# Fourth stage of a five-stage hybrid block: the product inside a chunk in 16-bit halves, ScalarE's input products, and a later output projection

## The chip, the cores and the metric

The kernel runs on one core of a Trainium2 chip. A core has TensorE (matrix products, into the eight PSUM banks), VectorE, ScalarE and GpSimd (elementwise work; GpSimd does not touch PSUM here) and a queue that starts DMAs. Each engine works through its own list of instructions in order and waits at semaphores for the others. The metric is the device time of one execution in microseconds (us), lower is better.

## The reference

The program applies five layers one after the other to 1024 tokens of 512 features: two scans over an image, a two-layer state-space block, a quantised linear layer, the state-space block that is changed here, and a mixture of experts. The changed layer computes this (`u` is the normalised input, 4 heads of 256 columns, state size 32):

```python
u_norm = u * jax.lax.rsqrt(jnp.mean(u * u, axis=-1, keepdims=True) + RMS_EPS) * norm_w
zxbcdt = u_norm @ in_proj_w.T + in_proj_b
...
dt = jax.nn.softplus(dt + dt_bias)
A = -jnp.exp(A_log)
dtA = jnp.exp(dt * A)
dtB = dt[..., None] * B_mat
def step(h, inp):
    dtA_t, dtB_t, x_t, C_t = inp
    h = h * dtA_t[:, :, None, None] + dtB_t[..., None] * x_t[:, :, None, :]
    y_t = jnp.einsum('bhn,bhnp->bhp', C_t, h)
    return (h, y_t)
...
y = y + x * D[None, None, :, None]
y = y.reshape(B, L, D_INNER)
y = y * jax.nn.silu(z)
return y @ out_proj_w.T + out_proj_b
```

## The kernel before

The five layers are five stages; every engine passes a common semaphore between two stages, so none starts a stage before all have ended the one before. All that follows is in the fourth, `stage_l3`, whose tiles have the prefix `ab_` in the profile. It holds the tokens in `t` and works through them in 8 chunks of 128, with the scan over time written as matrix products. `chunks` runs `body` for chunk 0, a loop over chunks 1 to 6, and chunk 7. There is one buffer of each tile for all chunks, and PSUM has a fixed use: bank 0 the output projection, bank 1 the projection to B and C and later the exponents, banks 2 and 3 x, the product inside the chunk and the transposed y, banks 4 and 5 z and the part from the state, banks 6 and 7 transposed B and C, B.C and the update of the state. The order on each engine is the order of the code; nothing else schedules it.

Big projections are done in halves: each 32-bit operand is the sum of two 16-bit tiles (`_hi`, `_lo`), and three 16-bit products (hi.hi, hi.lo, lo.hi) stand for one 32-bit product. Other products take 32-bit tiles as they are; the trace shows each of these as two records.

TensorE's list for a chunk, with the lines of the profile: transposes of B and C (L1679, 8); two products that give the differences of decay exponents (L1683, "the exponent product"); B.C per head (L1687, 4, only 32 rows deep); state times C (L1691, 4, 32 rows deep); the product inside the chunk, `M` times `xdt` (L1697, 4, 32-bit); the update of the state (L1702, 4, 32-bit); the next chunk's projection to B and C (L1644, 12 of 256 columns) and the first half of z (L1644, 12 of 512); transposes of y (L1712, 8); second half of z (12); the output projection (L1721, 24 of 512); the next chunk's x (L1644, 24 of 512).

Beside it, ScalarE copies the transposed B and C out (L1591), takes the exponential `E` (L1593), copies the transposed y out as its high half (L1595) and takes the tanh of z (L1580). VectorE masks B.C with the triangle (`gm`, L1478), forms `M = E * gm` (L1482), scales the state part (L1484), adds up y (L1489), gates it (L1491), adds to the state `S` (L1494), takes bc, the low half of y, z, the gate, the decays and x (L1438, L1498, L1442, L1446, L1457, L1451), multiplies x by dt (`xdt`, L1453), and last adds the output projection to `t` (L1510); the statistics of the chunk before are L1473. GpSimd forms `xe` (x times the decay to the chunk's end, L1612), `dx` (D times x, L1613), adds `dx` to y (L1617) and scales `S` (L1620).

## Time and profile before

| | us |
|---|---|
| runs: median (lowest, highest) | 1711.53 (1709.33, 1713.68), 3 runs |
| the profiled execution: its time | 1710.17 |
| the profiled execution: span of its instructions | 1708.4 |
| fourth stage, chunks 0 to 7 (917.3 to 1141.7 in the span) | 224.4 |
| TensorE busy in the whole span | 1363.5 (80%) |
| mean granted TensorE clock, whole span | 0.871 |

A page of the profile gives for each engine its busy time and, for groups of instructions of one line, their number, total and mean duration, and the idle time of the engine just before them with what ended it. The granted clock is a share of 2.4 GHz: 1.00 is that level, 0.50 is 1.2 GHz. Matrix products are pipelined: the duration of one has its way through the array in it, so in a dense row the distance from start to start counts, not the duration.

### The profile page before, as it was taken

What the parts mean: (1) busy time and instruction counts of PE and PEld (TensorE: products, weight loads), DVE (VectorE), ACT (ScalarE), POOL (GpSimd) and SP (SyncE); (2) the same over time, 40 slices, a digit from 0 to 9 for tenths busy, and PEclk for the clock granted to TensorE, in tenths of its full rate; (3) what the DMA queues carried; (4) which work ended last, traced back from release to release, by engine and by line L of the source; (5) the groups of instructions that cost most, each with busy time, mean ns of one, the idle gap of its engine ahead of it and who ended that gap; (6) DMA issues with size and microseconds to landing.
All of it is one profiled execution on the core that took longest, in us unless ns stands there. A gap on an engine that the chain in (4) does not pass through costs nothing.

```text
span 1708.4 us, 34435 instructions
## 1 busy us (share of the span) xinstructions
PE 1363.5 (80%) x12846; PEld 928.9 (54%) x12847; DVE 1109.4 (65%) x1669; ACT 671.5 (39%) x1011; POOL 417.0 (24%) x390
## 2 busy tenths in 40 slices
PE   3734889888548989884738999976699999999991
PEld 2214566665345666652425555544477777777770
DVE  3586877887578778876876555556456774667432
ACT  3236434344364343341252111124346664566330
POOL 0122333443313434432132323323100000000004
PEclk9757799999778899987858999885799999999996
DMA  8051000000220000003221000005543553535004
GB/s 293 18 173 61 2 2 1 1 1 1 80 82 2 2 1 1 1 1 105 93 83 50 0 0 0 0 4 209 193 183 142 218 217 114 218 126 219 25 25 153
DMA packets 34029, 132.30 MB, mean 77 GB/s; under 512 B 6665, under 2 KB 8457, under 8 KB 24017
## 3 DMA queue, kind: packets, MB, share of 16 engines
q1 hardware_dynamic: 25808, 103.19, 16.7%
q0 software_dynamic: 8160, 28.32, 4.9%
q8 instruction: 37, 0.61, 0.1%
q14 instruction: 24, 0.19, 0.0%
HBM read 108.82 MB, written 22.68 MB: 77 GB/s over the span
## 4 chain that ended last, share of the span: by engine, by line
PE 57%; DVE 24%; issue 7%; ACT 6%; DMA 4%; POOL 2%; DVEq 0%; POOLq 0%; SPq 0%; ACTq 0%
PE banks L2102 13%; PE banks L2123 13%; DVE mb_ca L592 8%; PE banks L1644 6%; PE banks L1003 5%; PE banks L1721 2%; PE banks L977 2%; PE banks L1040 2%; PE banks L1697 2%; PE banks L1050 2%; PE banks L1051 1%; ACT mb_ca L804 1%; POOL xs_table L2135 1%; DVE mb_xc L604 1%; DVE mb_y_lo L640 1%
## 5 line engine op out<-in xcount | busy, mean ns | idle before, releaser
L2102 PE MATMUL banks<-eb_x_hi,eb_w_hi 128*128 128x128 f16 x1344 | 228.3, 220 | 2.0 <-DVE eb_x_lo L2002 2.0
L2102 PE MATMUL banks<-eb_x_lo,eb_w_hi 128*128 128x128 f16 x1344 | 228.3, 220 | 0.0
L2102 PE MATMUL banks<-eb_x_hi,eb_w_lo 128*128 128x128 f16 x1344 | 228.3, 220 | 0.0
L977 PE MATMUL banks<-mb_u_hi,mb_wi_hi 128*128 (+3 forms) x1152 | 198.0, 220 | 3.3 <-ACT mb_ca L804 3.3
L977 PE MATMUL banks<-mb_u_hi,mb_wi_lo 128*128 (+3 forms) x1152 | 197.7, 220 | 0.0
L977 PE MATMUL banks<-mb_u_lo,mb_wi_hi 128*128 (+3 forms) x1152 | 197.6, 220 | 0.0
L592 DVE SCALAR_TENSOR_TENSOR mb_ca<-mb_xp,mb_par,mb_ca 128x128 f32<-128x128 f32 x384 | 162.9, 487 | 25.3 <-ACT mb_ca L804 23.3
L2102 PEld LDWEIGHTS banks<-eb_x_hi,eb_w_hi 128*128 128x128 f16 x1344 | 132.3, 98 | 4.8 <-issue 2.4
L2102 PEld LDWEIGHTS banks<-eb_x_lo,eb_w_hi 128*128 128x128 f16 x1344 | 132.3, 98 | 2.4
L2102 PEld LDWEIGHTS banks<-eb_x_hi,eb_w_lo 128*128 128x128 f16 x1344 | 132.3, 98 | 0.0
L2123 PE MATMUL banks<-eb_w_hi,eb_h_hi 128*128 x336 | 127.9, 381 | 0.4 <-issue 0.4
L2123 PE MATMUL banks<-eb_w_hi,eb_h_lo 128*128 x336 | 127.9, 381 | 0.0
L2123 PE MATMUL banks<-eb_w_lo,eb_h_hi 128*128 x336 | 127.9, 381 | 0.0
L977 PEld LDWEIGHTS banks<-mb_u_hi,mb_wi_hi 128*128 128x128 f16 (+1 forms) x1152 | 114.1, 99 | 9.4 <-issue 6.3
L1953 DVE TENSOR_TENSOR eb_hb<-banks,eb_b 128x512 f32<-128x512 f32 x84 | 57.4, 690 | 92.6 <-PE banks L2102 81.9
L977 PEld LDWEIGHTS banks<-mb_u_hi,mb_wi_lo 128*128 128x128 f16 (+1 forms) x1152 | 113.2, 98 | 1.7
L658 DVE TENSOR_TENSOR mb_M<-mb_E,banks 128x512 f32<-128x512 f32 x128 | 84.6, 683 | 44.5 <-ACT mb_E L851 44.5
L977 PEld LDWEIGHTS banks<-mb_u_lo,mb_wi_hi 128*128 128x128 f16 (+1 forms) x1152 | 113.2, 98 | 0.0
L851 ACT ACTIVATE mb_E<-banks 128x512 f32<-128x512 f32 x128 | 74.7, 597 | 91.0 <-PE banks L1051 87.8
L1992 DVE TENSOR_TENSOR eb_w_lo<-eb_raw,eb_w_hi 128x2048 f32 (+1 forms) x36 | 81.1, 2288 | 23.0 <-ACT eb_w_hi L1998 16.0
L2039 ACT ACT_TABLE_LOAD x21 | 26.9, 1283 | 170.4 <-DVE eb_hb L1953 170.4
L1960 DVE TENSOR_TENSOR eb_h_lo<-eb_hb,eb_h_hi 128x512 f16<-128x512 f32 x84 | 57.7, 687 | 37.8 <-ACT eb_h_hi L2041 37.6
(431 smaller groups left out, 3255.0 us busy)
## 6 DMA issues: line engine op xcount, KB each, us to landing
eb_raw<-e_w SPq DMA_DIRECT2D x36, 1024.0 KB, 4.8
eb_un<-e_w SPq DMA_DIRECT2D x28, 1024.0 KB, 7.2
mb_ring<-m_in_w SPq DMA_DIRECT2D x8, 1072.0 KB, 5.4
xs_table<-zero POOLq DMA_DIRECT2D x1, 6400.0 KB, 21.0
eb_xg<-xs_table POOLq DMA_DIRECT2D x23, 256.0 KB, 2.9
ys_table<-eb_y POOLq DMA_DIRECT2D x21, 256.0 KB, 6.5
ab_raw<-a_in_w SPq DMA_DIRECT2D x4, 1154.0 KB, 11.8
mb_ring<-m_out_w SPq DMA_DIRECT2D x4, 1024.0 KB, 5.3
```

Source lines behind the costliest of these rows:

```text
L592: x = e.scalar_tensor_tensor(out=ca[:, j, :], in0=xp[:, j, k:k + P], scalar=par[:, MB_CVW + 4 * j + k:MB_CVW + 4 * j + k + 1], in1=ca[:, j ...
L658: e.tensor_tensor(M[:, MB_HG * k:MB_HG * (k + 1), :], E[:, 512 * (k % MB_ER):512 * (k % MB_ER + 1)].rearrange("p (h t) -> p h t", h=MB_HG) ...
L851: e.activation(E[:, 512 * (k % MB_ER):512 * (k % MB_ER + 1)], ps[:, 3 + k % 2, :], ACT.Exp).then_inc(exped, 1)
L977: x = e.matmul(ps[0:width, bank, n * P:(n + 1) * P], a[:, k, f:f + width], b[:, k, ds(i * P, P)], start=(k == 0 and m == 0), stop=(k == KD ...
L1003: x = e.matmul(ps[:, 7, :], a[:, j, :], b[:, j, :], start=(j == 0 and m == 0), stop=(j == JD - 1 and m == 2))
L1040: x = e.transpose(ps[:, 5 + j // 4, (j % 4) * P:(j % 4 + 1) * P], xc[:, j, :], core.ident[:])
L1644: x = e.matmul(out, a[:, k, ds(i * P, P)], b[:, k, col:col + width], start=(k == 0 and m == 0), stop=(k == KD - 1 and m == 2))
L1953: e.tensor_tensor(hb[:, j % 2, :].rearrange("p (c n) -> p c n", c=EX_GB), ps[:, j, :].rearrange("p (c n) -> p c n", c=EX_GB), b1[:, ds(x, ...
L1960: e.tensor_tensor(h_lo[:, j, :], hb[:, j % 2, :], h_hi[:, j, :], ALU.subtract).then_inc(hlo_done, 1)
L1992: e.tensor_tensor(w_lo[:, side, n, :], raw[q], w_hi[:, side, n, :], ALU.subtract).then_inc(wlo_done, 1)
L2102: o = e.matmul(ps[:, j, c * P:(c + 1) * P], a[:, side, k, f * P:(f + 1) * P], b[:, k, :], start=(k == 0 and m == 0), stop=(k == KD - 1 and ...
L2123: o = e.matmul(ps[:, 5, :], a[:, j, c * P:(c + 1) * P], b[:, ds(side, 1), KD + j, c * D:(c + 1) * D].rearrange("p o c -> p (o c)"), start= ...
```

## The change

The product inside the chunk is made of halves: `M` and `xs` each get a 16-bit high half on ScalarE and a low half on VectorE, and 12 16-bit products take the place of 4 of 32 bits. The factor dt moves from x (`xdt` goes) into `gm`. `xe` and `dx` move from GpSimd to ScalarE, one instruction for each head; the addition of `dx` is folded into VectorE's scaling of the state part, which is four instructions now; GpSimd keeps the scaling of `S`. TensorE does a chunk's output projection one chunk later, between the next chunk's exponent product and its B.C (`out_project(g - 1)`); the last chunk's follows the loop. The next chunk's projection to B and C moves ahead of the state update, and the product inside the chunk behind it.

```diff
-    xs, xdt, xe, dx = (sb(n, [P, DI]) for n in ("xs", "xdt", "xe", "dx"))
+    M_hi, M_lo = sb("M_hi", [P, AT_HN, P], F16), sb("M_lo", [P, AT_HN, P], F16)
+    xs, xe, dx = (sb(n, [P, DI]) for n in ("xs", "xe", "dx"))
+    xs_hi, xs_lo = sb("xs_hi", [P, DI], F16), sb("xs_lo", [P, DI], F16)
...
-        def take_x(i, g):
+        def take_x(g):
             e.wait_ge(x_mm, g + 1)
             e.tensor_tensor(xs[:], two(2, 4), inb[:, AT_CX:AT_CX + DI], ALU.add).then_inc(x_done, 1)
-            e.wait_ge(x_done, g + 1)
-            e.tensor_tensor(hv(xdt[:]), hv(xs[:]), per_head(dt, i), ALU.mult).then_inc(xdt_done, 1)
...
+        def add_rows(i, g):
+            e.wait_ge(out_mm, g + 1)
+            e.scalar_tensor_tensor(out=t[:, i, :], in0=ps[:, 0, :], scalar=0.5, in1=t[:, i, :], op0=ALU.mult,
+                                   op1=ALU.add).then_inc(t_done, 1)
+
         def body(i, first, last):
             g = i
+            e.wait_ge(xhi_done, g + 1)
+            e.tensor_tensor(xs_lo[:], xs[:], xs_hi[:], ALU.subtract).then_inc(xlo_done, 1)
             e.wait_ge(g_mm, g + 1)
-            e.tensor_tensor(gm[:], ps[:, 6, :].rearrange("p (h t) -> p h t", h=AT_HN),
-                            core.tri[:].unsqueeze(1).to_broadcast([P, AT_HN, P]), ALU.mult).then_inc(gm_done, 1)
+            for h in range(AT_HN):
+                x = e.scalar_tensor_tensor(out=gm[:, h, :], in0=ps[:, 6, h * P:(h + 1) * P], scalar=dt[:, i, h:h + 1],
+                                           in1=core.tri[:], op0=ALU.mult, op1=ALU.mult)
+            x.then_inc(gm_done, 1)
             e.wait_ge(gm_done, g + 1)
             e.wait_ge(exped, g + 1)
             e.tensor_tensor(M[:], E[:], gm[:], ALU.mult).then_inc(m_done, 1)
+            e.wait_ge(mhi_done, g + 1)
+            e.tensor_tensor(M_lo[:], M[:], M_hi[:], ALU.subtract).then_inc(mlo_done, 1)
             e.wait_ge(inter_mm, g + 1)
-            e.tensor_tensor(hv(y1[:]), hv(two(4, 6)), per_head(ecum, i), ALU.mult).then_inc(y1_done, 1)
+            e.wait_ge(dx_done, g + 1)
+            for h in range(AT_HN):
+                x = e.scalar_tensor_tensor(out=head(y1, h), in0=ps[:, 4 + h // 2, (h % 2) * AT_HW:(h % 2 + 1) * AT_HW],
+                                           scalar=ecum[:, i, h:h + 1], in1=head(dx, h), op0=ALU.mult, op1=ALU.add)
+            x.then_inc(y1_done, 1)
             if not first:
-                statistics(i - 1, g - 1)
+                add_rows(i - 1, g - 1)
+            e.wait_ge(y1_done, g + 1)
             e.wait_ge(intra_mm, g + 1)
-            e.wait_ge(y3_done, g + 1)
             e.tensor_tensor(y1[:], y1[:], two(2, 4), ALU.add).then_inc(y2_done, 1)
             e.wait_ge(y2_done, g + 1)
             e.tensor_tensor(y[:], y1[:], sz[:], ALU.mult).then_inc(y_done, 1)
...
                 take_bc(g + 1)
+            if not first:
+                statistics(i - 1, g - 1)
             e.wait_ge(yhi_done, g + 1)
             e.tensor_tensor(yT_lo[:], two(2, 4), yT_hi[:], ALU.subtract).then_inc(ylo_done, 1)
...
-                take_x(i + 1, g + 1)
-            e.wait_ge(out_mm, g + 1)
-            e.scalar_tensor_tensor(out=t[:, i, :], in0=ps[:, 0, :], scalar=0.5, in1=t[:, i, :], op0=ALU.mult,
-                                   op1=ALU.add).then_inc(t_done, 1)
+                take_x(g + 1)
 
         e.wait_ge(bias_added, 1)
         chunks(e, body)
+        add_rows(TT - 1, TT - 1)
...
+        e.wait_ge(prep, 1)
...
+            e.wait_ge(x_done, g + 1)
+            e.activation(xs_hi[:], xs[:], ACT.Copy).then_inc(xhi_done, 1)
+            for h in range(AT_HN):
+                x = e.activation(head(xe, h), head(xs, h), ACT.Copy, scale=dte[:, i, h:h + 1])
+            x.then_inc(xe_done, 1)
+            for h in range(AT_HN):
+                x = e.activation(head(dx, h), head(xs, h), ACT.Copy, scale=dpar[:, h:h + 1])
+            x.then_inc(dx_done, 1)
+            e.wait_ge(m_done, g + 1)
+            e.activation(M_hi[:], M[:], ACT.Copy).then_inc(mhi_done, 1)
             e.wait_ge(yt_mm, g + 1)
             e.activation(yT_hi[:], two(2, 4), ACT.Copy).then_inc(yhi_done, 1)
...
-            e.wait_ge(x_done, g + 1)
-            e.tensor_tensor(hv(xe[:]), hv(xs[:]), per_head(dte, i), ALU.mult).then_inc(xe_done, 1)
-            e.tensor_tensor(hv(dx[:]), hv(xs[:]), dpar[:].unsqueeze(2).to_broadcast([P, AT_HN, AT_HW]), ALU.mult)\
-                .then_inc(dx_done, 1)
-            e.wait_ge(y1_done, g + 1)
-            e.wait_ge(dx_done, g + 1)
-            e.tensor_tensor(y1[:], y1[:], dx[:], ALU.add).then_inc(y3_done, 1)
+            e.wait_ge(inter_mm, g + 1)
...
+        def out_project(g):
+            e.wait_ge(ylo_done, g + 1)
+            for j in range(JD):
+                for m, (a, b) in enumerate(((yT_hi, wo_hi), (yT_hi, wo_lo), (yT_lo, wo_hi))):
+                    x = e.matmul(ps[:, 0, :], a[:, j * P:(j + 1) * P], b[:, j, :], start=(j == 0 and m == 0),
+                                 stop=(j == JD - 1 and m == 2))
+            x.then_inc(out_mm, 1)
...
             x.then_inc(diff, 1)
+            if not first:
+                out_project(g - 1)
             e.wait_ge(bct_done, g + 1)
             for h in range(AT_HN):
...
-            e.wait_ge(xdt_done, g + 1)
-            e.wait_ge(m_done, g + 1)
-            for h in range(AT_HN):
-                x = e.matmul(ps[:, 2 + h // 2, (h % 2) * AT_HW:(h % 2 + 1) * AT_HW], M[:, h, :], xdt[:, h * AT_HW:(h + 1) * AT_HW],
-                             start=True, stop=True)
-            x.then_inc(intra_mm, 1)
+            if not last:
+                e.wait_ge(exped, g + 1)
+                project_bc(i + 1)
             e.wait_ge(xe_done, g + 1)
+            e.wait_ge(gm_done, g + 1)
             for h in range(AT_HN):
                 x = e.matmul(ps[0:NS, 6 + h // 2, (h % 2) * AT_HW:(h % 2 + 1) * AT_HW], bc[:, 2 * h * NS:(2 * h + 1) * NS],
                              xe[:, h * AT_HW:(h + 1) * AT_HW], start=True, stop=True)
             x.then_inc(ds_mm, 1)
+            e.wait_ge(xlo_done, g + 1)
+            e.wait_ge(mlo_done, g + 1)
+            core.apart(e)
+            for h in range(AT_HN):
+                for m, (a, b) in enumerate(((M_hi, xs_hi), (M_hi, xs_lo), (M_lo, xs_hi))):
+                    x = e.matmul(ps[:, 2 + h // 2, (h % 2) * AT_HW:(h % 2 + 1) * AT_HW], a[:, h, :], head(b, h),
+                                 start=(m == 0), stop=(m == 2))
+            x.then_inc(intra_mm, 1)
             if not last:
-                project_bc(i + 1)
                 e.wait_ge(y1_done, g + 1)
                 project_z(i + 1, 0)
             e.wait_ge(y_done, g + 1)
@@ -1711,20 +1750,15 @@
             for j in range(JD):
                 x = e.transpose(ps[:, 2 + j // 4, (j % 4) * P:(j % 4 + 1) * P], y[:, j * P:(j + 1) * P], core.ident[:])
             x.then_inc(yt_mm, 1)
+            if not first:
+                e.wait_ge(t_done, g)
             if not last:
                 project_z(i + 1, 1)
-            e.wait_ge(ylo_done, g + 1)
-            if not first:
-                e.wait_ge(t_done, g)
-            for j in range(JD):
-                for m, (a, b) in enumerate(((yT_hi, wo_hi), (yT_hi, wo_lo), (yT_lo, wo_hi))):
-                    x = e.matmul(ps[:, 0, :], a[:, j * P:(j + 1) * P], b[:, j, :], start=(j == 0 and m == 0),
-                                 stop=(j == JD - 1 and m == 2))
-            x.then_inc(out_mm, 1)
-            if not last:
+                e.wait_ge(ylo_done, g + 1)
                 project_x(i + 1)
 
         chunks(e, body)
+        out_project(TT - 1)
```

The places where the lists of instructions differ, as far as the prediction speaks of them. TensorE, before, a chunk inside the loop (what stands after L1702 are the projections to B and C, z, the transposes, z, output projection, x):

```order
L1679 MATMUL banks<-ident,ab_bc 32x128 x8
L1683 MATMUL banks<-ab_r_hi,after 128x512
L1683 MATMUL banks<-ab_r_lo,after 128x512
L1687 MATMUL banks<-ab_bct 128x128 x4
L1691 MATMUL banks<-ab_S,ab_bct 128x256 x4
L1697 MATMUL banks<-ab_xdt,ab_M 128x256 x4
L1702 MATMUL banks<-ab_xe,ab_bc 32x256 x4
```

The same place in the changed kernel (L1698 is the first of the 24 products of the output projection, L1668 of the 12 for B and C, L1742 stands four times three):

```order
L1715 MATMUL banks<-ab_r_hi,after 128x512
L1715 MATMUL banks<-ab_r_lo,after 128x512
L1698 MATMUL banks<-ab_wo_hi,ab_yT_hi 128x512
...
L1721 MATMUL banks<-ab_bct 128x128 x4
L1725 MATMUL banks<-ab_S,ab_bct 128x256 x4
...
L1668 MATMUL banks<-ab_wi_hi,ab_u_hi 128x256
...
L1734 MATMUL banks<-ab_xe,ab_bc 32x256 x4
L1742 MATMUL banks<-ab_xs_hi,ab_M_hi 128x256
L1742 MATMUL banks<-ab_xs_lo,ab_M_hi 128x256
L1742 MATMUL banks<-ab_xs_hi,ab_M_lo 128x256
```

The output projection has moved between the exponent product and B.C; B.C and state times C still stand next to each other, with the B and C projection behind them and the product inside the chunk last. VectorE, before, from B.C to the end of y:

```order
L1478 TENSOR_TENSOR ab_gm<-banks,tri 128x512
L1482 TENSOR_TENSOR ab_M<-ab_E,ab_gm 128x512
...
L1484 TENSOR_TENSOR ab_y<-banks,ab_ecum 128x1024
...
L1489 TENSOR_TENSOR ab_y<-ab_y,banks 128x1024
L1491 TENSOR_TENSOR ab_y<-ab_y,ab_sz 128x1024
```

And in the changed kernel:

```order
L1487 TENSOR_TENSOR ab_xs_lo<-ab_xs,ab_xs_hi 128x1024
...
L1490 SCALAR_TENSOR_TENSOR ab_gm<-banks,ab_dt,tri 128x128
...
L1495 TENSOR_TENSOR ab_M<-ab_E,ab_gm 128x512
L1497 TENSOR_TENSOR ab_M_lo<-ab_M,ab_M_hi 128x512
...
L1501 SCALAR_TENSOR_TENSOR ab_y<-banks,ab_ecum,ab_dx 128x256
...
L1481 SCALAR_TENSOR_TENSOR t_res<-banks,t_res 128x512
L1508 TENSOR_TENSOR ab_y<-ab_y,banks 128x1024
L1510 TENSOR_TENSOR ab_y<-ab_y,ab_sz 128x1024
```

Two low halves are new, the two scalings have become four instructions each, and the addition to `t` now stands ahead of the last two steps of y.

## Rows read from the trace of the kernel before

**Rows 1.** Busy time by stretch: chunks 1, 2 and 7, sum of all eight.

```profile
core 0: us, PE busy (x) PEld busy (x) DVE busy (x) ACT busy (x) POOL busy (x), PEclk, DMA share, GB/s
945.60:973.60 28.00, 27.22 (x135) 15.39 (x134) 15.66 (x16) 3.57 (x4) 9.31 (x4) 0.94 0.00 1
973.60:1003.30 29.70, 29.03 (x135) 16.15 (x134) 15.66 (x16) 3.57 (x4) 9.41 (x4) 0.89 0.00 0
1119.40:1141.70 22.30, 16.84 (x75) 9.77 (x73) 13.00 (x11) 2.52 (x3) 8.90 (x4) 0.85 0.00 1
sum 224.40, PE 213.48 PEld 120.19 DVE 120.94 ACT 27.52 POOL 73.68; mean PE 26.69 PEld 15.02 DVE 15.12 ACT 3.44 POOL 9.21
```

**Rows 2.** Chain that ended last, chunk 3: start us, us, what.

```profile
1008.66 3.44 PE banks L1697 x8
1012.11 1.84 PE banks L1702 x8
1013.95 4.01 PE banks L1644 x24
1017.96 0.87 PE banks L1712 x8
1018.83 2.59 PE banks L1644 x12
1021.42 5.18 PE banks L1721 x24
1026.60 5.18 PE banks L1644 x24
```

**Rows 3.** Timeline, chunk 3: start us, us, engine, line, work [idle before <-releaser].

```profile
1003.33 1.04 PE L1679 MATMUL banks<-ident,ab_bc 128*32 128x128 f32 x8
1003.63 1.22 DVE L1451 TENSOR_TENSOR ab_xs<-banks,ab_inb 128x1024 f32<-128x1024 f32 x1 [5.61 <-PE banks L1644]
1004.40 1.01 ACT L1591 ACTIVATE ab_bct<-banks 32x1024 f32<-32x1024 f32 x1 [8.85 <-PE banks L1679]
1005.47 1.15 PE L1687 MATMUL banks<-ab_bct 32*128 32x128 f32 x8 [0.67 <-ACT ab_bct L1591]
1006.47 1.89 PE L1691 MATMUL banks<-ab_S,ab_bct 32*128 32x256 f32 x8
1008.66 3.44 PE L1697 MATMUL banks<-ab_xdt,ab_M 128*128 128x256 f32 x8 [0.31 <-DVE ab_M L1482]
```

**Rows 4.** Granted clock (PEclk) by stretch, in chunks 3, 2 and 0.

```profile
1005.50:1008.20 2.70, 2.70 (x16) 2.27 (x16) 2.67 (x4) 0.40 (x1) 2.70 (x2) 1.00 0.00 0
1008.20:1011.70 3.50, 3.19 (x8) 2.52 (x8) 2.12 (x3) 0.00 (x0) 3.35 (x2) 0.51 0.00 0
977.50:984.30 6.80, 6.80 (x17) 4.10 (x16) 3.91 (x5) 0.00 (x0) 6.33 (x4) 0.50 0.00 0
919.50:922.30 2.80, 2.80 (x17) 2.28 (x17) 1.50 (x4) 0.38 (x1) 2.60 (x2) 1.00 0.00 0
922.90:926.30 3.40, 3.40 (x10) 1.90 (x9) 0.70 (x1) 0.00 (x0) 3.26 (x2) 0.50 0.00 0
```

**Rows 5.** Prices of single operations, by line or from the timeline.

```profile
L1482 DVE TENSOR_TENSOR ab_M<-ab_E,ab_gm x8: 693/1066/1066, 921.4 to 1125.2; 128x512 f32<-128x512 f32 x8
L754 ACT ACTIVATE mb_wo_hi<-mb_ring,mb_par x16: 705/707/722, 137.0 to 490.5; 128x512 f16<-128x512 f32 x16
639.65 1.14 DVE L592 SCALAR_TENSOR_TENSOR mb_ca<-mb_xp,mb_par,mb_ca 128x128 f32<-128x128 f32 x4
1007.93 2.34 POOL L1613 TENSOR_TENSOR ab_dx<-ab_xs,ab_dpar 128x1024 f32<-128x1024 f32 x1
```

**Rows 6.** Timeline of chunk 7, from the sum of y to the output projection.

```profile
1130.19 1.22 DVE L1489 TENSOR_TENSOR ab_y<-ab_y,banks 128x1024 f32<-128x1024 f32 x1 [2.20 <-PE banks L1697]
1132.88 1.06 PE L1712 MATMUL banks<-ident,ab_y 128*128 128x128 f32 x8 [0.39 <-DVE ab_y L1491]
1133.98 1.02 ACT L1595 ACTIVATE ab_yT_hi<-banks 128x1024 f16<-128x1024 f32 x1 [12.03 <-PE banks L1712]
1136.32 0.39 PE L1721 MATMUL banks<-ab_wo_hi,ab_yT_hi 128*128 128x512 f16 x1 [2.38 <-DVE ab_yT_lo L1498]
```

More of the change, by code:

```diff
@@ L1351, in stage_l3 @@
         sums_exp prep bias_added zeroed bc_mm x_mm z_mm bc_done x_done z_ev thz_done sz_done bct_mm bct_done g_mm
[L1352 to L1353 removed]
+        r_done diff gm_done exped m_done mhi_done mlo_done inter_mm y1_done smul ds_mm s_done intra_mm xhi_done xlo_done
+        xe_done dx_done y2_done y_done yt_mm yhi_done ylo_done out_mm t_done""".split()
     s = {n: sem(n) for n in names}
```

11 lines of the change are left out of this document (6 added, 5 removed).

## The prediction

> **What bounds the kernel now.** I first read busy time by stretch [rows 1]. The eight chunks of the fourth stage take 224.4 us, and TensorE is busy for 213.5 of them; VectorE has 15.66 us of work in a chunk of 28 to 29.7 us, ScalarE 3.57, GpSimd 9.4. The chain that ended last [rows 2] says the same step by step: inside the stage it is TensorE's list almost without a break. So the stage gets shorter only by what TensorE's list gets shorter, as long as nobody makes it wait anew. Then I read the timeline of one chunk [rows 3] for TensorE's few idle times: 0.67 us before B.C (L1687), while ScalarE copies the transposed B and C out, and 0.31 us before the product inside the chunk (L1697), while VectorE forms M. Last I read the clock [rows 4]. It is at 2.4 GHz (1.00) while B.C and state times C run, and at 1.2 GHz (0.50) right after, while the product inside the chunk runs: for 3.4 us in chunks 0 and 3, for 6.8 us in chunk 2. The reader is to see three removable things: a product that takes 3.44 us in chunk 3, idle time, and a clock that falls at the same place in every chunk.
>
> **TensorE's list in a chunk of the loop, after.** Distances from start to start, in the order of the new list:
> - transposes of B and C 0.87, priced as the equal eight of L1712 [rows 2], and exponent product 2 x 0.216, a 512-column product being 5.18 / 24 = 0.216 [rows 2]: 1.30
> - output projection of the chunk before, 24 products: 5.18 [rows 2]
> - B.C 1.00 (1005.47 to 1006.47) and state times C 1.85 (1006.47 to 1008.66 without 0.31 idle and the end of the pipeline) [rows 3]: 2.85
> - projection to B and C: the 24 products of L1644 in 4.01 less 12 wide ones in 2.59 [rows 2]: 1.42
> - state update: 1.84 [rows 2]
> - product inside the chunk, 12 16-bit products of 256 columns, which is the form and the number of the projection to B and C: 1.42
> - first half of z 2.59, transposes 0.87, second half of z 2.59, x 5.18 [rows 2]: 11.23
>
> That is 25.24 us. The product inside the chunk is the one step that gets cheaper: 3.44 before, 1.42 now. No row shows that product at full clock; the state product of equal width took 1.85 there, so the split alone may be worth only 0.4 us and the clock the rest, which is why the clock decides more than the arithmetic.
>
> **Waits.** B.C now waits for ScalarE's copy behind 5.18 us of output projection. The copy ends at 1005.41, 2.08 after the first transpose [rows 3], and B.C's turn comes at 1.30 + 5.18 = 6.5: the 0.67 idle goes; its cover is the projection, and without it (chunk 0) the wait stays. The output projection's own input, the low half of y, is already needed before x is projected, so it is there.
>
> The new chain to the low half of M, counted from the chunk's first transpose: B.C is visible at about 7.65 (1.15 after its start [rows 3]). Four maskings with a scalar: 1.14, the price of the four equal 128x128 instructions on VectorE [rows 5]. M: 0.69 with GpSimd idle, 1.07 with it busy [rows 5]; GpSimd waits for the state product now, so 0.69. ScalarE's high half of 512 columns lies between half of its 1.01 for 1024 [rows 3] and 0.71 with a scale [rows 5]; I take 0.6. The low half 0.69 to 1.07. With handovers the chain ends at 11.0 to 11.4. TensorE comes to the product after 1.30 + 5.18 + 2.85 + 1.42 + 1.84 = 12.6, so 1.2 to 1.6 us of cover are left, by the B and C projection and the state update.
>
> ScalarE takes on nine instructions of x: one of 1024 columns (1.0 [rows 3]) and eight of 256 columns with a scale. For those I have 0.71 at 512 columns as upper bound and a fourth of 1.01, 0.25, as lower; I take 0.4. They start when the exponential ends, at about 2.6, and end at 2.6 + 1.0 + 8 x 0.4 = 6.8 (9.3 at the upper bound). The high half of M is asked for at 9.5: still free. The state update wants xe at 10.75 and VectorE's scaling wants dx at 11: both there. Queued on VectorE behind its new wait for the high half of xs (3.7) is only the masking, which cannot start before 7.65. GpSimd loses 2.34 [rows 5] for dx, as much for the addition, and xe; nobody waits for the scaling of S before the end of y.
>
> VectorE ends the chunk's y. After M_lo come four scalings of 256 columns (about 1.6 against 1.22), then the addition to t (0.7), ending at 13.5; the product inside the chunk is visible at 12.6 + 1.42 + 0.2 = 14.2. Then from the start of the sum of y to TensorE's transposes is 2.69 us (1130.19 to 1132.88 [rows 6]), so they can start at 16.9. TensorE reaches them at 12.6 + 1.42 + 2.59 = 16.6. A new wait of about 0.25 us: before, 4.01 us of projections [rows 2] stood there, now 2.59. From the transposes to the low half of y are 3.44 us (1132.88 to 1136.32 [rows 6]); TensorE has 0.87 + 2.59 = 3.46 in between, so x waits for nothing, with no slack at all.
>
> Chunk period: 25.24 + 0.25 = 25.5.
>
> **The sum at full clock.** Before, chunks 1 to 6 took 224.4 - 28.3 (chunk 0) - 22.3 (chunk 7) = 173.8 us [rows 1], 29.0 each; after, 6 x 25.5 = 153.0: -20.8. Chunk 0 has no projection to do and nothing to cover its waits: 25.5 - 5.18 + 0.67, plus 0.2 for the low half of M and 0.2 more for VectorE's scaling, 21.4 against 28.3: -6.9. Chunk 7 gets a projection more: 1.30 + 5.18 + 2.85 + 1.84 = 11.2, product inside the chunk to 12.6; VectorE's addition to t now stands in the way until 13.5; then 6.13 us to the start of the last projection (1130.19 to 1136.32 [rows 6]) and 5.3 for it: 24.9 against 22.3, +2.6. Together -25.1. Outside the chunks the change only takes xdt from chunk 0's approach and lets ScalarE wait for dte there, which I count as nothing: both fall under TensorE's first transposes.
>
> **The clock.** In chunk 0, 919.50 to 922.30, TensorE was busy for 2.80 of 2.80 us with B.C and state times C, and at 922.90 the clock was at 0.50 [rows 4]. So no idle gap is needed: those two shallow 32-bit products are enough for it to fall. They still stand together, 2.85 us long. What is new is what surrounds them: 5.18 us of 16-bit products ahead where in chunk 3 there was 0.67 us of nothing, 1.42 us behind. A mean of 0.94 over the 28 us of chunk 1 [rows 1] is 3.4 us at half and nothing more, so the dense 16-bit part of the chunk never lost the clock. I expect it to fall in about half of the chunks, four, depending on how it meets the pair. A fall costs half of the 3.4 us that it lasted in chunk 0 [rows 4], 1.7 us: +6.8. That makes -18.3, and 1711.5 - 18.3 = **1693 us** (the profiled execution was 1710.2, so 1692 against that; its span is 1.8 shorter than its time).
>
> The Trainium skill says otherwise ("TensorE: Matmul & The Clock Gate", section "Why this matters for your kernels"): drops in the middle of a kernel come from gaps in which TensorE idles between bursts. By that rule no chunk of the new kernel would lose the clock, and the sum is that of the first rival. The trace does not bear it out: no idle of rows 3 is longer than 0.67 us, and the clock fell. A second rule speaks against the change: multiplications belong on VectorE, not ScalarE ("ScalarE: Activation LUTs", section "Rules for kernel authors"). By it the eight scalings would be a loss; here ScalarE has about 25 us free in a chunk [rows 1] and VectorE is the one in the chain, so I do not follow it.
>
> **Rivals.**
> 1. The clock stays up in all chunks, because the idle ahead of the pair is gone. For it: in chunks 2 and 3 idle did stand ahead. Against it: chunk 0. 1711.5 - 25.1 = 1686 us.
> 2. The clock falls in each chunk as before. For it: the pair is unchanged, and every chunk before has a mean of 0.94 or less, as in rows 1. 8 x 1.7 = 13.6: 1711.5 - 11.5 = 1700 us.
> 3. The chain over the halves of M, or that to the low half of y, is late: each has its point at 1.2 and 0 us. If each 16-bit handover were 0.3 us slower than I count, y's two chains would cost some 0.6 us in seven chunks on top of the forecast: 1697 us; with 1 us and more, 1702.
> 4. Slower than before: ScalarE becomes the bound. Its eight scalings stand ahead of the high half of M; from (9.5 - 3.6) / 8 = 0.74 us each on they delay it, from 0.9 they delay TensorE. To eat the whole gain of 3.5 us in a chunk they would have to take 1.35 each, twice the 512-column row. At 1.5 each it would be 8 x (1.5 - 1.35) x 7 = 8 us over: 1720 us. Only a cost for scalars addressed by a register in the loop, of which these rows show nothing, could do it.
>
> **Chances.** Forecast (two to six falls) 0.55; rival 1 0.18; rival 2 0.15; rival 3 0.09; rival 4 0.03. The range 1683 to 1701 takes in rivals 1 and 2 and 3 us for the price of the ScalarE and VectorE steps at the low end; it leaves out the worse part of rival 3 and rival 4. A measurement of this kernel tells about 0.3%, 5 us, from no change. Faster by more: 0.95; within: 0.03; slower: 0.02.
>
> **What will show it.** The product inside the chunk at 1.4 us (right) or 2.6 (clock at half there); chunk period near 25.5 with PEclk 1.00 or near 27.2 with about 0.93; TensorE's idle before B.C gone but for chunk 0, and a new one of 0.2 to 0.3 us before the transposes of y; ScalarE at some 8 us in a chunk. It would be wrong if ScalarE's 256-column scalings exceed 0.74 us, if TensorE waits for the low half of M in the loop, or if the time after the stage changes, since nothing there is touched.

## The result and the profile after

| | us |
|---|---|
| runs: median (lowest, highest) | 1697.89 (1689.26, 1699.11), 6 runs |
| the kernel before beside it | 1711.5 (1708.32, 1713.96), 6 runs |
| ratio after to before | 0.9909, 95% interval 0.9883 to 0.9934 |
| the profiled execution: time, span | 1697.89, 1696.3 (before 1710.17, 1708.4) |
| fourth stage, chunks 0 to 7 (914.0 to 1124.1) | 210.0 (before 224.4) |

The kernel is 13.6 us faster; 18.5 were forecast, and 1697.9 lies in the range of 1683 to 1701.

The page of the kernel after: busy time, share and instructions of each engine over the whole span, and the granted clock in 40 slices.

```profile
span 1696.3 us, 34671 instructions
...
PE 1351.3 (80%) x12878; PEld 917.7 (54%) x12879; DVE 1122.3 (66%) x1725; ACT 709.9 (42%) x1091; POOL 358.7 (21%) x366
...
PEclk9757899998778999987878999975899999999996
```

Next, busy time by stretch, as in [rows 1, 4]. The stretches are chunk 1, chunk 2, B.C and state times C of chunk 2, what stands right behind them, chunk 6, chunk 7, and chunk 7 from the transposes of y on.

```profile
core 0: us, PE busy (x) PEld busy (x) DVE busy (x) ACT busy (x) POOL busy (x), PEclk, DMA share, GB/s
936.00:961.60 25.60, 25.45 (x140) 14.05 (x139) 17.45 (x23) 8.34 (x14) 1.88 (x1) 1.00 0.00 1
961.60:988.70 27.10, 26.96 (x139) 14.63 (x138) 17.46 (x23) 8.34 (x14) 1.89 (x1) 0.94 0.00 0
968.10:971.10 3.00, 3.00 (x19) 2.44 (x19) 1.62 (x5) 0.16 (x1) 0.00 (x0) 1.00 0.00 0
971.30:974.70 3.40, 3.40 (x15) 1.79 (x13) 2.71 (x4) 0.63 (x1) 1.79 (x1) 0.51 0.00 0
1070.30:1095.80 25.50, 25.36 (x140) 14.00 (x139) 17.45 (x23) 8.34 (x14) 1.88 (x1) 1.00 0.00 0
1095.80:1124.00 28.20, 21.83 (x103) 11.17 (x101) 13.40 (x18) 7.29 (x13) 1.88 (x1) 0.88 0.00 0
1113.50:1124.10 10.60, 8.05 (x25) 2.92 (x24) 1.83 (x3) 1.02 (x1) 0.00 (x0) 0.68 0.00 0
```

A chunk without a fall of the clock takes 25.55 us, one with a fall 27.17; the fall comes right behind the shallow pair, with TensorE busy for 3.00 of 3.00 us there and 26.96 of 27.10 in the whole chunk. ScalarE has 8.34 us in a chunk (before 3.57), VectorE 17.45 (before 15.66), GpSimd 1.88 (before 9.3).

The chain that ended last, chunk 3, which answers to [rows 2] (start us, us, what):

```profile
988.89 0.87 PE banks L1711 x8
989.76 0.43 PE banks L1715 x2
990.20 5.18 PE banks L1698 x24
995.38 1.08 PE banks L1721 x8
996.46 1.73 PE banks L1725 x8
998.19 2.29 PE banks L1668 x12
1000.47 2.60 PE banks L1734 x8
1003.08 1.43 PE banks L1742 x12
...
1004.60 1.23 DVE ab_y L1508
...
1005.86 1.24 DVE ab_y L1510
...
1007.23 1.06 PE banks L1751 x8
```

The new product inside the chunk (L1742) takes 1.43 us where L1697 took 3.44. The low clock now lies on the projection to B and C (2.29 for 1.42) and the state update (2.60 for 1.84). The same chunk in the timeline, VectorE, ScalarE and GpSimd around M:

```profile
997.77 0.69 DVE L1495 TENSOR_TENSOR ab_M<-ab_E,ab_gm 128x512 f32<-128x512 f32 x1
...
998.37 1.88 POOL L1644 TENSOR_TENSOR ab_S<-ab_S,ab_edec 32x1024 f32<-32x1024 f32 x1 [25.28 <-PE banks L1725]
...
998.50 0.63 ACT L1623 ACTIVATE ab_M_hi<-ab_M 128x512 f16<-128x512 f32 x1 [3.07 <-DVE ab_M L1495]
...
999.16 1.64 DVE L1497 TENSOR_TENSOR ab_M_lo<-ab_M,ab_M_hi 128x512 f16<-128x512 f32 x1 [0.69 <-ACT ab_M_hi L1623]
```

Last, the chain of chunk 7, which answers to [rows 6]:

```profile
1109.86 1.22 DVE ab_y L1508
...
1112.47 1.08 PE banks L1751 x8
...
1113.57 1.03 ACT ab_yT_hi L1625
...
1114.63 1.24 DVE ab_yT_lo L1519
...
1116.00 8.03 PE banks L1698 x24
```

The last output projection takes 8.03 us; [rows 2] have 5.18 for the same 24 products. It runs for its greater part at 0.50: the fall goes from 1114.6 to 1121.4.

**The stage, kernel by kernel.** Each number is the distance from one chunk's first transpose of B and C to the next one's, in the profiled execution; the last runs to the end of the last output projection. A fall is a stretch of 3.4 us at 0.50; a double one is 6.8 us long.

| kernel | chunk 0 | chunks 1 to 6 | chunk 7 | sum | falls in chunks 0 to 6 |
|---|---|---|---|---|---|
| before | 28.1 | 28.2, 29.7, 28.3, 29.7, 28.3, 29.7 | 22.3 | 224.4 | in each; 3 of them double |
| after | 22.0 | 25.6, 27.2, 27.2, 27.2, 27.2, 25.6 | 28.2 | 210.0 | 4 |
| after_again | 22.0 | 25.6, 27.2 x5 | 27.6 | 211.0 | 5 |
| pair_apart | 22.3 | 25.7 x6 | 27.6 | 204.3 | 0 |
| old_pair_apart | 27.2 | 27.4 x6 | 22.3 | 213.6 | 0 |
| old_apart_17 | 29.0 | 27.4 x6 | 22.3 | 215.3 | 0 |
| product32 | 21.7 | 26.1, 27.6, 26.1 x3, 27.7 | 28.5 | 209.7 | 2 |
| out_old_place | 27.2 | 27.2 x3, 29.6, 27.9, 29.6 | 25.1 | 221.1 | 3; 2 of them double |
| old_out_moved | 22.9 | 27.4 x6 | 26.8 | 213.8 | in each, single |
| gpsimd_products | 22.8 | 25.5 x6 | 27.6 | 203.6 | 1, in chunk 0 |
| shift_09 | 22.9 | 25.5, 27.2 x3, 25.5 x2 | 27.6 | 208.7 | 3 |
| shift_17 | 23.8 | 27.2 x6 | 27.6 | 214.4 | 6 |
| filled_end | 22.0 | 25.5, 27.2 x5 | 25.5 | 208.9 | 5 |
| apart_filled | 22.3 | 25.7 x6 | 25.9 | 202.6 | 0 |

The stage went down by 14.3 us. What lies before and after it is the same code in all these kernels, but for the few instructions next to the stage, and still differs: chunk 0 starts between 911.6 and 919.7, and the time behind the stage is 564.3 to 574.6. From before to after these were -3.3 and +5.6, so -14.3 becomes -12.0 in the span (1708.4 to 1696.3). That is why small differences are read from the stage, not from one execution's time.

The traces show what goes with these differences: the time that the same code spends at half clock. Behind the stage apart_filled has 100.9 us at 0.50 and takes 564.3, before 108.5 and 566.7, after 112.7 and 572.3, gpsimd_products 119.4 and 574.6, and the other ten lie along the same line. Ahead of the stage before has 293.5 us at 0.50 and after 286.7, and the stage starts 3.3 us earlier.

### The profile page after: what moved, and what is told of

It is laid out like the page before. It is cut to its first block, busy times and chain, and to the rows that moved or that the text cites. A ratio compares the mean times of both kernels' runs of the same rounds, so it can differ in the third digit from the quotient of the medians.

```text
span 1696.3 us, 34671 instructions
## 1 busy us (share of the span) xinstructions
PE 1351.3 (80%) x12878; PEld 917.7 (54%) x12879; DVE 1122.3 (66%) x1725; ACT 709.9 (42%) x1091; POOL 358.7 (21%) x366
## 4 chain that ended last, share of the span: by engine, by line
PE 55%; DVE 25%; issue 7%; ACT 6%; DMA 4%; POOL 2%; DVEq 0%; POOLq 0%; SPq 0%; ACTq 0%
PE banks L2136 13%; PE banks L2157 13%; DVE mb_ca L592 8%; PE banks L1003 5%; PE banks L1668 5%; PE banks L1698 3%; PE banks L977 2%; PE banks L1040 2%; PE banks L1050 2%; PE banks L1051 1%; ACT mb_ca L804 1%; POOL xs_table L2169 1%; DVE mb_xc L604 1%; DVE mb_y_lo L640 1%; DMA eb_un<-ys_table,eb_slot 1%
```

## The experiments

The theory: the shallow pair, B.C and state times C in a row, makes the clock fall; the split, the moved work and ScalarE's products are worth what TensorE's list says. The rivals: the fall comes from idle time ahead of B.C; or the gain comes from the output projection's new place alone.

### The pair taken apart in the new kernel (pair_apart)

```diff
             x.then_inc(g_mm, 1)
+            if not last:
+                e.wait_ge(exped, g + 1)
+                project_bc(i + 1)
             e.wait_ge(z_ev, g + 1)
...
-            if not last:
-                e.wait_ge(exped, g + 1)
-                project_bc(i + 1)
             e.wait_ge(xe_done, g + 1)
```

> The changed kernel, with the projection to B and C moved between B.C and state times C, so that the two shallow 32-bit products no longer stand next to each other. Theory (the pair in a row is what makes the clock fall): the four falls in the loop go, every chunk takes 25.5 us at PEclk 1.00, the kernel some 7 us less than the changed one, 1691 us. Rival (the clock falls for the 32-bit work of the chunk as a whole, or for the small waits): chunks of 27.2 us remain, at least three of them, and the time stays at 1698 us.

Measured: 1692.32 (1687.42 to 1698.21, 5 runs), ratio to before 0.9917, 0.989 to 0.9944. Busy time by stretch, two loop chunks and a part of chunk 7 (columns here and below as in the table of busy time after):

```profile
933.90:959.60 25.70, 25.56 (x139) 14.06 (x138) 16.60 (x23) 8.34 (x14) 1.88 (x1) 1.00 0.00 1
1036.90:1062.60 25.70, 25.56 (x140) 14.08 (x138) 16.60 (x23) 8.34 (x14) 1.88 (x1) 1.00 0.00 0
1105.40:1112.10 6.70, 4.24 (x14) 1.89 (x13) 2.34 (x3) 1.02 (x1) 0.00 (x0) 0.50 0.00 0
```

No chunk of the loop loses the clock. The chunk is 0.19 us longer than the undisturbed one of after and 1.4 shorter than the disturbed one; the stage is 204.3 us, 5.8 less than in after. In whole time the two cannot be told apart (0.9917 and 0.9909). In chunk 7, where nothing is put between the pair, the clock falls as in after, but 17.1 us behind the first transpose and so behind the idle 3.13 us, not behind the pair. By itself this run is weak evidence, since gpsimd_products, below, kept the pair together and had no fall in the loop either.

### The same in the old kernel (old_pair_apart)

```diff
             x.then_inc(g_mm, 1)
+            if not last:
+                e.wait_ge(exped, g + 1)
+                project_bc(i + 1)
             e.wait_ge(z_ev, g + 1)
...
             if not last:
-                project_bc(i + 1)
                 e.wait_ge(y1_done, g + 1)
```

> The kernel before, with only that same move: its projection to B and C from behind the state update to between B.C and state times C. Theory of the pair: the clock no longer falls once or twice in every chunk, the 32-bit product inside the chunk takes about 1.9 us where it took 3.4 to 3.8, chunks fall from 29.0 to about 27 us, the kernel to about 1697 us. Rival (the 0.67 us of idle before B.C makes it fall, which this kernel keeps): PEclk of 0.94 and 0.89 in the chunks as before, 1711 us.

Measured: 1696.81 (1694.39 to 1702.32, 8 runs), ratio 0.9933, 0.9914 to 0.9951. A loop chunk by busy time, and its wait ahead of B.C in the timeline:

```profile
944.90:972.30 27.40, 26.32 (x136) 14.39 (x135) 15.66 (x16) 3.57 (x4) 9.30 (x4) 1.00 0.00 1
```

```profile
974.42 1.15 PE L1687 MATMUL banks<-ab_bct 32*128 32x128 f32 x8 [0.67 <-ACT ab_bct L1591]
...
978.84 1.99 PE L1700 MATMUL banks<-ab_xdt,ab_M 128*128 128x256 f32 x8
```

The idle of 0.67 us of [rows 3] is still there, and the clock does not fall in any of chunks 0 to 6; the 32-bit product inside the chunk takes 1.99 us where it took 3.44. So the idle ahead of B.C is not enough to cause a fall. One call in another place takes 10.7 us from the stage, three quarters of what the whole change took.

### Was the point of time lucky? (old_apart_17, shift_09, shift_17, after_again)

The kernel after, run once more with nothing changed:

> The changed kernel once more, unchanged, for a second profile. Theory (how many chunks lose the clock hangs on how the chunk meets it, not on the code): the chunks are again 25.5 or 27.2 us long and nothing between, but their number may be another than four. Rival: again exactly chunks 2 to 5.

It took 1695.61 (one run), with five falls where the first profile had four.

Extra products in chunk 0 of after, whose result is overwritten, shift all chunks behind by 0.9 us (four products) or 1.7 us (eight):

```diff
             if not first:
                 e.wait_ge(t_done, g)
+            if first:
+                for _ in range(4):
+                    e.matmul(ps[:, 0, :], u_hi[:, 0, 0:P], wi_hi[:, 0, 0:512], start=True, stop=True)
             if not last:
                 project_z(i + 1, 1)
```

> The changed kernel with four 512-column 16-bit products more in chunk 0, just ahead of the second half of z; nobody reads them. The loop is not touched, it only starts 0.9 us later than in the changed kernel. Theory (a chunk falls or not by the moment at which its shallow pair comes, relative to the moments at which the granted clock can change): the row of falls in chunks 2 to 5 breaks, at most two of chunks 1 to 6 have a fall, the rest take 25.5 us. Rival (what counts is only what surrounds the pair): four or five chunks of 27.2 us, as in both profiles of the changed kernel.

> The same with eight such products, 1.7 us. Theory: now chunk 1's pair comes at the bad moment, and since a chunk with a fall is 27.2 us long and the falls of the changed kernel stand 27.3 us apart, each brings the next one along: falls from chunk 1 on, in at least four chunks in a row, no chunk in between at 25.5. Rival: the first fall again in chunk 2, four or five in all.

Measured in one run each: 1697.81 and 1695.9. Chunks 1, 2 and 5 of shift_09 and chunk 1 of shift_17, by busy time:

```profile
942.60:968.10 25.50, 25.36 (x140) 13.99 (x139) 17.45 (x23) 8.34 (x14) 1.88 (x1) 1.00 0.00 1
968.10:995.30 27.20, 27.06 (x140) 14.70 (x139) 17.46 (x23) 8.34 (x14) 1.88 (x1) 0.94 0.00 0
1049.60:1075.20 25.60, 25.45 (x140) 14.07 (x139) 17.45 (x23) 8.33 (x14) 1.88 (x1) 1.00 0.00 0
```

```profile
935.80:962.90 27.10, 26.95 (x139) 14.66 (x138) 17.46 (x23) 8.34 (x14) 1.88 (x1) 0.94 0.00 1
```

Shift_17 has a fall in each chunk from 1 to 6. Shift_09 has three, one more than was allowed for. The falls form a regular row: in after, after_again, filled_end and the two shifts every loop fall begins 9.4 to 10.1 us behind its chunk's first transpose, and the pair ends at about 9.3 (998.19 - 988.89). The falls are 27.3 us apart and a chunk with one is 27.17 us long, so a chunk hit once is followed by others hit 0.13 us later, and each row ends at about 10.1 us behind the first transpose or with the loop. How many chunks fall therefore hangs on when the first one is met.

That raises a doubt about old_pair_apart: its chunk of 27.35 us meets such a row at one point only, and may have been lucky. So it got the shift too:

```diff
             if not first:
                 e.wait_ge(t_done, g)
+            if first:
+                for _ in range(8):
+                    e.matmul(ps[:, 0, :], u_hi[:, 0, 0:P], wi_hi[:, 0, 0:512], start=True, stop=True)
             for j in range(JD):
```

> The kernel before with B.C apart from the state product (the edit of old_pair_apart), and eight more 512-column products in chunk 0 ahead of its output projection, whose result is overwritten: they shift all chunks behind by 1.7 us against the point at which the clock fell elsewhere. Its chunk period of 27.35 us is close to the 27.3 us between falls, so without a shift it meets the clock at one point only, and luck is not excluded. Theory (the pair in a row causes the falls): again no fall in chunks 1 to 6, periods 27.3 to 27.4; chunk 0 some 1.5 us longer than 27.2; stage near 215. Rival (only the point of time decides, as the shifts of the changed kernel might suggest): a fall in every chunk from 1 on, as where the output projection alone was moved, periods of 27.4 with it or 28 to 29; stage near 217 to 225.

Measured: 1701.86 (1697.83 to 1706.74, 10 runs), ratio 0.9957, 0.994 to 0.9975. Its chunk 1:

```profile
944.90:972.30 27.40, 26.32 (x136) 14.41 (x135) 15.67 (x16) 3.57 (x4) 9.31 (x4) 1.00 0.00 1
```

Again no fall in chunks 0 to 6. With pair_apart and apart_filled that makes four kernels, 24 loop chunks, with the pair apart and not one fall.

The last chunk of this kernel is its own control, for there the pair stands together. Its stretch of the pair, then what follows:

```profile
1111.50:1114.30 2.80, 2.69 (x16) 2.10 (x15) 2.80 (x3) 0.23 (x1) 2.80 (x2) 0.99 0.00 0
1114.30:1121.10 6.80, 4.91 (x11) 3.06 (x12) 4.57 (x6) 0.00 (x0) 5.04 (x3) 0.50 0.00 0
```

The fall begins 5.1 us behind the first transpose. Counted back from it by 27.3 us at a time, the same moment lies 5.1 to 5.3 us behind the first transpose in each of chunks 1 to 6, and there, with the pair apart, nothing falls. With the pair together falls began at such points elsewhere: at 5.0 and 5.5 us in chunks 5 and 7 of out_old_place, at 5.6 in chunk 0 of before, at 5.5 in chunk 7 of old_pair_apart. This, more than the count of 24, speaks against luck in the old kernel. For pair_apart and apart_filled there is no such control in the loop.

The kernel is 5 us longer than old_pair_apart, of which the stage explains 1.7; the rest lies outside it (behind the stage the profiled executions have 570.9 and 568.1) or in the spread of the runs.

### The product left at 32 bits (product32)

`M_hi`, `M_lo`, `xs_hi`, `xs_lo` and the 12 products go; all else stays as in the change.

```diff
-            e.wait_ge(xlo_done, g + 1)
-            e.wait_ge(mlo_done, g + 1)
-            core.apart(e)
+            e.wait_ge(m_done, g + 1)
             for h in range(AT_HN):
-                for m, (a, b) in enumerate(((M_hi, xs_hi), (M_hi, xs_lo), (M_lo, xs_hi))):
...
+                x = e.matmul(ps[:, 2 + h // 2, (h % 2) * AT_HW:(h % 2 + 1) * AT_HW], M[:, h, :], head(xs, h), start=True, stop=True)
```

> The changed kernel with the product inside the chunk in 32 bits again, at its new place; the halves of M and xs are not made. It measures the term that no row before showed. Theory: at full clock the product takes 1.85 us, as state times C does, so the split is worth only 0.4 us a chunk, chunks without a fall are 25.9 us, the kernel some 3 to 4 us slower than the changed one, 1701 us. Rival (the split itself is the gain): the product takes 2.5 us or more at full clock and the kernel comes to 1706 us or above.

Measured: 1695.87 (1692.04 to 1697.94, 5 runs), ratio 0.9918, 0.9892 to 0.9944. The chain of its chunk 2:

```profile
973.37 2.67 PE banks L1659 x12
976.04 2.17 PE banks L1725 x8
978.22 1.94 PE banks L1730 x8
```

The 32-bit product takes 1.94 us at full clock against 1.43 split: 0.5 us, which is also the difference of the undisturbed chunks (26.05 and 25.55). Seven chunks make 3.5 us. I had forecast 1701 us for the kernel; in whole time it cannot be told apart from after. Its profiled execution met only two falls, against four.

### The output projection in its old place (out_old_place)

```diff
             x.then_inc(diff, 1)
-            if not first:
-                out_project(g - 1)
             e.wait_ge(bct_done, g + 1)
...
+            if not last:
+                project_z(i + 1, 1)
             if not first:
                 e.wait_ge(t_done, g)
+            out_project(g)
             if not last:
-                project_z(i + 1, 1)
-                e.wait_ge(ylo_done, g + 1)
                 project_x(i + 1)
```

VectorE's addition to `t` goes back to the end of the chunk as well.

> The changed kernel with the output projection at its old place, between the second half of z and x, and the addition to t at the end of VectorE's chunk. Theory: the 0.67 us wait before B.C is back in every chunk and with it nothing dense stands ahead of the pair, so that the clock falls in every chunk: 26.2 + 1.7 = 27.9 us a chunk, while the last chunk is 5 us shorter and the first as much longer; the kernel at about 1704 us. Rival (the place of the projection only hides the copy): 4 falls as before, 0.7 us a chunk more, 1702 us, and the same number of chunks at PEclk 1.00 as in the changed kernel.

Measured: 1709.57 (1702.06 to 1713.98, 10 runs), ratio 0.9998, 0.9977 to 1.0019: the rest of the change, without this move, gains nothing that can be measured in whole time (in the stage it is 3.3 us). Chunk 2 by busy time, then its timeline:

```profile
968.80:996.00 27.20, 25.62 (x139) 13.94 (x138) 17.53 (x23) 8.34 (x14) 1.88 (x1) 1.00 0.00 0
```

```profile
970.97 1.15 PE L1717 MATMUL banks<-ab_bct 32*128 32x128 f32 x8 [0.67 <-ACT ab_bct L1609]
...
972.38 1.23 DVE L1487 TENSOR_TENSOR ab_xs_lo<-ab_xs,ab_xs_hi 128x1024 f16<-128x1024 f32 x1 [1.42 <-ACT ab_xs_hi L1613]
...
973.52 1.12 DVE L1490 SCALAR_TENSOR_TENSOR ab_gm<-banks,ab_dt,tri 128x128 f32<-128x128 f32 x4
...
974.67 1.81 DVE L1495 TENSOR_TENSOR ab_M<-ab_E,ab_gm 128x512 f32<-128x512 f32 x1
...
977.97 0.27 PE L1738 MATMUL banks<-ab_xs_hi,ab_M_hi 128*128 128x256 f16 x1 [0.85 <-issue]
```

I had forecast 26.2 us for a chunk, the list and the 0.67 us of idle; an undisturbed one took 27.2. The missing 1.0 us is the chain to M's low half. B.C is there at about 972.1, but VectorE takes up the low half of xs at 972.38 and gets to the masking at 973.52; then M takes 1.81 us beside GpSimd's scaling of S. TensorE waits 0.85 us ahead of the product. So the projection's place covers two waits, that for B and C and that for M. Chunks 0 to 3 of this kernel have the idle of 0.67 us and no fall, where I had forecast one in every chunk: this idle does not bring one by itself, and nor does the pair, which stands together there.

### The projection moved alone in the old kernel (old_out_moved)

The edit is the reverse of the one above, made in before: `out_project(g - 1)` between the exponent product and B.C, the addition to `t` and the statistics later; the 32-bit product, `xdt` and GpSimd's products stay.

> The kernel before with the output projection's move alone (the addition to t and the statistics at their new places); products, GpSimd and ScalarE as before. Theory: the 0.67 us ahead of B.C go, and the 5.2 us of dense products ahead of the pair spare some chunks the clock's fall: chunks of 26.0 us without and 27.7 to 28 with one, where before all had one or two; the kernel at about 1699 us. Rival (the move only hides the copy): every chunk 0.7 us shorter with its falls kept, 28.3 us on average, the kernel at 1706 us.

Measured: 1691.61 (1690.26 to 1695.67, 4 runs), ratio 0.9907, 0.9882 to 0.9932. Its chunk 1:

```profile
934.90:962.30 27.40, 27.40 (x136) 15.24 (x135) 15.38 (x16) 3.57 (x4) 8.86 (x4) 0.94 0.00 1
```

TensorE is busy without any gap, and still the clock falls once in each chunk; the double falls of before are gone. I had forecast that some chunks would be spared, and 1699 us. The stage takes 213.8 us, 10.6 less than before. On whole time the one move is as good as the whole change (0.9907 and 0.9909).

### ScalarE's input products back on GpSimd (gpsimd_products)

```diff
-            for h in range(AT_HN):
-                x = e.activation(head(xe, h), head(xs, h), ACT.Copy, scale=dte[:, i, h:h + 1])
-            x.then_inc(xe_done, 1)
...
+            e.tensor_tensor(hv(xe[:]), hv(xs[:]), per_head(dte, i), ALU.mult).then_inc(xe_done, 1)
```

and `dx` in the same way.

> The changed kernel with xe and dx back on GpSimd, whole (two instructions for eight). Theory (ScalarE's input products are off the critical path and gain nothing by themselves): xe at 4.6 and dx at 6.9 us after the chunk's start are still early enough, chunks without a fall stay at 25.5 us, the kernel within 2 us of the changed one. Rival (GpSimd's work slows VectorE's chain to the halves of M and the move is part of the gain): chunks without a fall at 26 us or more, the kernel at 1702 us or above.

Measured: 1693.37 (1685.93 to 1694.09, 4 runs), ratio 0.9891, 0.9864 to 0.9918. Its chunk 2:

```profile
962.50:988.00 25.50, 25.36 (x139) 13.99 (x138) 17.45 (x23) 5.15 (x6) 6.70 (x3) 1.00 0.00 0
```

The chunk is 25.54 us, the same as an undisturbed one of after: it does not matter which of the two engines does these products. The shallow pair stands together here and the loop has no fall, but chunk 0 has one, at 919.8. Counted on by 27.3 us it would be 947.1, 10.2 us behind chunk 1's first transpose, just past the 9.4 to 10.1 at which falls of the loop begin. That the first chunk's other length gave another meeting, as with the shifts, is likely, but not shown by a run of its own. I do not count these 6.4 us of the stage as a gain of the edit.

### Filling TensorE's idle time in the last chunk (filled_end, apart_filled)

Where chunks 0 to 6 project the next chunk's z, chunk 7 projects its own once more and throws the result away:

```diff
+            e.wait_ge(y1_done, g + 1)
             if not last:
-                e.wait_ge(y1_done, g + 1)
                 project_z(i + 1, 0)
+            else:
+                project_z(i, 0)
...
                 project_x(i + 1)
+            else:
+                project(i, ps[:, 5, :], 512, 512)
```

Apart_filled has this and the edit of pair_apart.

> The changed kernel; in the last chunk TensorE computes that chunk's z a second time, half by half, where the loop has the next chunk's z, and nobody reads it (24 products of added work in time that was idle). Theory (in the changed kernel the clock is low during the last output projection because TensorE idles 3.1 and 2.4 us before it): the projection takes 5.3 us and not 8.0, the last chunk 25.5 us and not 28.2, the kernel about 3 us less, 1695 us; falls in the loop stay. Rival (the low clock there comes from the pair before it): the last chunk stays at 28 us.

> Both at once: the projection to B and C between B.C and state times C, and z once more in the last chunk. If both theories hold, no chunk has a fall: 22.2 + 6 x 25.7 + 25.5 = 202 us for the eight chunks, against 210 in the changed kernel and 224.4 before; the kernel at 1688 us, 10 us under the changed one. If the falls merely move elsewhere, the sum stays above 205 us.

Measured: filled_end 1687.11 (1680.42 to 1693.17, 4 runs), ratio 0.9856, 0.9821 to 0.989; apart_filled 1686.41 (1680.12 to 1688.99, 5 runs), ratio 0.9863, 0.9841 to 0.9884. Chunk 7 of the first, then of the second:

```profile
1099.70:1125.20 25.50, 24.36 (x128) 12.97 (x127) 13.94 (x19) 7.29 (x13) 1.88 (x1) 1.00 0.00 1
```

```profile
1088.30:1114.20 25.90, 25.76 (x127) 13.38 (x125) 13.49 (x18) 7.29 (x13) 1.88 (x1) 0.93 0.00 1
```

With 24 products more (5.2 us at the 0.216 of [rows 2]) the last chunk of filled_end is 2.7 us shorter than in after, 2.1 shorter than the 27.6 of after_again: the clock stays up, and the last output projection runs at it. Here idle time was the cause. In apart_filled, against the expectation, chunk 7 has a fall (the 0.93): it lasts 3.4 us and begins at 1098.4, 10.1 us behind the first transpose and right behind the pair, which stands together in this chunk. The last projection runs at full clock there too. Apart_filled is the fastest of all in the stage, 202.6 us. The interval of its ratio, 0.9841 to 0.9884, begins well below that of after, 0.9883 to 0.9934, and ends where that begins; each ratio is to the kernel before in runs beside it (1708.6 us here, 1711.5 beside after). Filled_end cannot be told apart from it in whole time, nor, by the interval, clearly from after.

## Why the prediction was right, and where it was off

**The loop: right to the tenth.** Forecast 25.5 us for a chunk at full clock and 27.2 with a fall, four falls: chunks 1 to 6 at 6 x 25.5 + 6.8 = 159.8 us. Measured 25.55 and 27.17, four falls, 159.8. Before, chunks 1 to 6 took 174.0 and chunk 0 28.1; I had 173.8 and 28.3, which leaves the sum as it is. The split product is 1.43 us (1.42 forecast), the eight scalings of ScalarE start 0.40 us apart (0.4 forecast), and the idle before B.C is gone but for chunk 0. The wait ahead of the transposes of y is 0.15 us (25.45 of 25.60 busy), with 0.25 forecast.

**The number of falls: right, with luck in it.** The mechanism, that the shallow pair needs no idle time to make the clock fall, is shown from both sides: four kernels with the pair parted have no fall in the loop, though two of them keep the idle, and old_out_moved has no idle and a fall in each chunk. The pair is needed for these falls but does not bring one each time: with it together, loops had 0 to 6. The four was an even guess between the rivals, and the same kernel had five the next time. My reason for fewer falls, dense work around the pair, is not borne out: old_out_moved has the same 5.18 us of products ahead of the pair and a fall in every chunk, out_old_place has 0.67 us of nothing there and none in four chunks. Rivals 1 and 2 are both ends that occur: 0 falls in the loop in gpsimd_products, 6 in shift_17.

The rule weighed in the prediction, of the Trainium skill ("TensorE: Matmul & The Clock Gate", section "Why this matters for your kernels"), puts drops in the middle of a kernel down to idle gaps between bursts of products. In the loop the trace does not agree: TensorE is busy for 27.40 of 27.40 us in old_out_moved and the clock falls. In chunk 7 of after it agrees: TensorE idles 3.13 us ahead of the transposes of y, 2.46 ahead of the last projection, and the fall goes when they are filled. I set the rule aside for the whole stage when only rows of chunks 0 to 3 had spoken against it.

**Chunk 7: the term that failed, +3.3 us.** Forecast 13.5 to the sum of y, 6.13 to the projection, 5.3 for the projection: 24.9. Measured 14.1 (1109.86 - 1095.80), 6.14 and 8.03: 28.2. I priced the last projection at full clock, with the two idle stretches ahead of it in my own sum. In before the fall of chunk 7 had come earlier, under the 32-bit product, and the projection ran at full clock (1136.32 to 1141.7); a fall over it costs 2.7 us (2.1 in after_again, whose last chunk took 27.6). Filled_end shows it: with the idle filled the last chunk takes 25.5. The other 0.6 us is M's low half, which took 1.66 and not 0.69 to 1.07, with no projection here to cover it.

**Chunk 0: +0.6 us.** Forecast 21.4, measured 22.03. TensorE waited 0.81 us ahead of the product, not 0.2. What I took as queued harmlessly on VectorE, the low half of xs, stands ahead of the masking until 918.79, when B.C is there at 917.3, since in chunk 0 no projection delays B.C. Then M runs beside GpSimd's scaling of S and takes 1.70 us. Out_old_place shows the same chain in each chunk.

**Rival 3 was nearer than I wrote.** M's low half took 1.64 us in the loop (the timeline of chunk 3 after), since GpSimd scales S at that time; I had GpSimd waiting for the state product, which it does; but that product ends at 998.2, and the scaling, from 998.37 on, lies just on M's halves. The low half ends at 948.1 in chunk 1 and TensorE asks at 948.7: 0.5 to 0.6 us of cover, where I had counted 1.2 to 1.6.

**Sum.** -25.1 at full clock and +6.8 for four falls made -18.3. With +3.3 for chunk 7 and +0.6 for chunk 0 it is -14.4, and the stage measured -14.3. The times before and behind the stage, which I had as unchanged, moved by -3.3 and +5.6, and a change behind the stage was one of my signs of being wrong. That the whole time still landed in the range is in part luck: the two nearly cancel, and by more or fewer falls outside the stage they differ by several us between kernels. Behind it the trace of after has a fall for 3.4 us at 1210.2 that before has not, and the time at 0.50 there goes with the length of that part in all the traces, as said above; but why the falls there differ stays open, since no run here was made for it.

**ScalarE.** A page of the Trainium skill ("ScalarE: Activation LUTs", section "Rules for kernel authors") gives multiplications to VectorE. I did not follow it for lack of room on VectorE. That they do no harm on ScalarE is right; gpsimd_products shows that the move brought nothing either, since GpSimd, once freed of the addition of `dx`, does them just as well in 4.8 us a chunk (6.70 less 1.88 busy). No run here put them on VectorE.

**What the change is made of, in the stage.** The projection's move gave most: without it 221.1 us, alone 213.8. Chunks of the loop with a fall compare best, 27.17 in after and 27.36 where the move stands alone, so that the rest of the change is worth 0.2 us in such a chunk, and most of what after is ahead in the loop (159.8 to 164.1) is its two chunks without a fall. The split is worth 0.5 us in a chunk at full clock. The falls that are left cost 1.6 us each, and apart_filled is 7.4 us below after by parting the pair and filling the end.

## What to carry to other kernels

Where a row of the trace shows the clock at half behind a pair of shallow products with TensorE busy throughout, try other ready products between the two before anything is split or moved: in the old kernel one moved call took 10.7 us from this stage. Price the last turn of a loop by itself, with the clock that its idle stretches leave, as work that covered a wait in the loop is not there. Judge such a change by several executions and by the stage's own rows, since the count of falls, 3 to 6 for the same loop in four traces, moves the stage by up to 5 us without any gain of the edit.
